# A seven-product block scheme for a quarter-size piece of the main product, with W0 read from DRAM again in every batch

## The chip, the cores and the metric

One core of one Trainium2 chip runs the kernel as a single program. The metric is the device time of one execution in microseconds (us). Five engines matter: PE (matmuls), DVE and ACT (elementwise work, both can read PSUM), POOL (elementwise work in SBUF, and DMAs of its own) and SP (issues most of the DMAs). They run their instruction lists in order and meet at semaphores.

## The reference

Four layers, each added to its input. `x` is 8 batches x 256 tokens x 1024.

```python
# layer 0: a plain weight, and a sign matrix of its own for every batch
x = x + (einsum('bsi,oi->bso', x, W0) + b0 + einsum('bsi,bio->bso', x, 2*mask - 1) * coeff[:, None, None])
# layer 1: a weight that is quantized to a codebook, with a LoRA part
x = x + x @ w_eff.T
# layer 2: a shared weight, bias, and an adapter per batch, chosen by token
x = x + (einsum('bti,oi->bto', x, W2) + b2 + lora(x, A2[tok2[b]], B2[tok2[b]]) * 2.0)
# layer 3: a rank-16 adapter per batch
x = x + einsum('bnr,bor->bno', einsum('bni,bri->bnr', x, B3[tok3[b]]), A3[tok3[b]])
```

## The kernel before

The first 175 us or so build what all batches share. Layers 1 and 2 with their residuals are one 1024x1024 matrix P = (I + W1eff)^T (I + W2)^T, kept as a high part `P_hi` and a low part `P_lo`, both float32r; a product of two such pairs is three matmuls (high-high, high-low, low-high). W0^T plus the identity is written to `w0t_dram` in DRAM and read into SBUF once, as `w0_t` (32 KB of each partition).

Then come eight batches. A batch has two halves on PE.

*Layer 0* (lines 1432 and 1439). The mask arrives as eight row tiles k = 0 to 7, each 128 partitions x 1024 (two k-tiles of 512 output columns), in a ring of four slots. For each row tile ACT turns the mask into signs (`signs`, L730, 1024 wide), DVE adds the tile of W0 (`merged`, L1078, 1024 wide), ACT rounds each half to float32r (`m_hi`, L740, 512 wide, twice) and DVE takes the rest (`m_lo`, L1084, 512 wide, twice). `Mh` and `Ml` are rings of four halves, so a half n waits until PE is through with half n-4. PE works on pairs of halves: eight matmuls of 512 columns with `m_hi` (both halves), then eight of 256 columns with `m_lo`. Halves n = 2k and 2k+1 are row tile k. The output of layer 0 goes through `x1_part` (ACT, L777), `x1_sum` (DVE, L1131), `x1_hi` (ACT, L781) and `x1_lo` (POOL for four tiles, DVE for four).

*Main* (lines 1468 to 1470). Four outputs (2 token halves x 2 column halves of 512) are each the sum over eight k-tiles of three matmuls, 96 matmuls in all. Between them stand eight `rank` matmuls (L1478) and, at the end of each output, one `close` matmul with the adapters (L1485). `out_add` on DVE (L1127) adds the bias to the bank and writes `out_staged` (two slots), and SP stores it.

The order on every engine is written out by hand. ACT stands in `signs(4)`, `signs(5)`, `m_hi(2)`, `m_hi(3)`, `m_hi(4)`, `signs(6)`, `m_hi(5)`, four `x1_part`, `m_hi(6)`, `signs(7)`, `m_hi(7)`. SP issues masks, tables, `x` and stores from one in-order queue, each behind its own wait: mask tile k+4 goes out when `m_lo(k)` has freed the slot, and the next batch's `x` when layer 0 has been read.

Of the kernel before, what the change touches and what calls it, by code (L numbers as in the profile page):

```python
# [30 lines left out]
def cond_resid_chain(nc, x, coeff, codebook, tok2, tok3, mask, w0, b0, w1, scale_log, lora_a, lora_b,  # L31
# [161 lines left out]
    with ExitStack() as ctx:  # L193
        def sem(name):
# [27 lines left out]
        MAIN_BANK = [3, 6, 7, 4]  # L222
        RANK_BANK = 5
# [36 lines left out]
        def _(sp):  # L260
# [1266 lines left out]
```

## Time and profile before

| | |
|---|---|
| median of 3 runs | 557.57 us (557.49 to 558.6) |
| the profiled execution's own time | 557.65 us |
| its span (first to last instruction) | 555.6 us |
| PE busy | 541.3 us, 97% of the span |
| DVE, ACT, POOL busy | 398.2, 328.9 and 157.8 us (72%, 59%, 28%) |
| moved by DMA | 80.07 MB, 144 GB/s over the span |

The profiled execution's time is its span and 2.05 us around it, and it is 0.08 us above the median of the runs. A PE matmul is shown longer than its turn takes, since matmuls overlap: the turn is read from the starts of two that follow each other. A busy share is an average over stages; what an edit in one stage can bring is read from the waits of that stage.

### The profile page before, as it was taken

What the parts mean: (1) busy time and instruction counts of PE and PEld (TensorE: products, weight loads), DVE (VectorE), ACT (ScalarE), POOL (GpSimd) and SP (SyncE); (2) the same over time, 40 slices, a digit from 0 to 9 for tenths busy, and PEclk for the clock granted to TensorE, in tenths of its full rate; (3) what the DMA queues carried; (4) which work ended last, traced back from release to release, by engine and by line L of the source; (5) the groups of instructions that cost most, each with busy time, mean ns of one, the idle gap of its engine ahead of it and who ended that gap; (6) DMA issues with size and microseconds to landing.
All of it is one profiled execution on the core that took longest, in us unless ns stands there. A gap on an engine that the chain in (4) does not pass through costs nothing.

```text
span 555.6 us, 8876 instructions
## 1 busy us (share of the span) xinstructions
PE 541.3 (97%) x2892; PEld 464.6 (84%) x2892; DVE 398.2 (72%) x622; ACT 328.9 (59%) x622; POOL 157.8 (28%) x170
## 2 busy tenths in 40 slices
PE   5999999999999999999999999999999999999997
PEld 4988888888888788888888888888888888888886
DVE  5998898988956859666765875866687487586631
ACT  3877766776655846564564664656557466564620
POOL 2769778987714040021012002102100300210200
PEclk9999999999999999999999999999999999999999
DMA  8766042733577982574475366256447635634202
GB/s 230 246 88 143 21 145 62 248 97 113 120 192 231 314 204 97 170 186 69 149 221 113 132 187 156 63 170 197 76 151 226 114 119 163 174 73 151 76 0 76
DMA packets 138120, 80.07 MB, mean 144 GB/s; under 512 B 95664, under 2 KB 111024, under 8 KB 138096
## 3 DMA queue, kind: packets, MB, share of 16 engines
q1 hardware_dynamic: 137520, 78.71, 51.8%
q0 software_dynamic: 288, 1.05, 0.5%
q8 instruction: 13, 0.21, 0.2%
q14 instruction: 11, 0.09, 0.0%
q10 hardware_dynamic: 288, 0.01, 0.0%
HBM read 65.59 MB, written 14.16 MB: 144 GB/s over the span
## 4 chain that ended last, share of the span: by engine, by line
PE 84%; DVE 8%; ACT 4%; DMA 3%; issue 1%; POOL 0%; DVEq 0%; ACTq 0%; SPq 0%; POOLq 0%
PE bank L1432 19%; PE bank L1468 10%; PE bank L1469 10%; PE bank L1470 10%; PE bank L1439 10%; PE bank L1306 5%; PE bank L1308 5%; PE bank L1307 5%; PE bank L1478 3%; PE bank L1216 2%; PE bank L1485 1%; DVE merged_ring L1078 1%; DVE w_lo L984 1%; DMA mask_ring<-in_mask_Bx4096x_ik 1%; ACT bank L574 1%; PE bank L1230 1%
## 5 line engine op out<-in xcount | busy, mean ns | idle before, releaser
L1432 PE MATMUL bank<-x_t_pair,m_hi 128*128 128x512 f32 x512 | 128.4, 393 | 1.8 <-ACT m_hi L740 1.6
L740 ACT CAST m_hi<-merged_ring 128x512 fp32r<-128x512 f32 x128 | 73.0, 618 | 66.1 <-PE bank L1439 34.1
L1432 PEld LDWEIGHTS bank<-x_t_pair,m_hi 128*128 128x128 f32 x512 | 92.5, 189 | 19.5 <-ACT m_hi L740 2.6
L1084 DVE TENSOR_TENSOR m_lo<-merged_ring,m_hi 128x512 fp32r<-128x512 f32 x128 | 82.4, 689 | 30.7 <-ACT m_hi L740 30.6
L1468 PE MATMUL bank<-P_hi,x_t_pair 128*128 128x512 f32 x256 | 99.7, 389 | 0.0
L1469 PE MATMUL bank<-P_lo,x_t_pair 128*128 128x512 f32 x256 | 99.7, 389 | 0.0
L1470 PE MATMUL bank<-P_hi,x_t_pair 128*128 128x512 f32 x256 | 99.6, 389 | 0.0
L530 POOL TENSOR_TENSOR x_t_pair<-x_sum,x_t_pair 128x256 fp32r<-128x256 f32 x32 | 24.8, 801 | 260.5 <-ACT x_t_pair L781 260.5
L1078 DVE TENSOR_TENSOR merged_ring<-merged_ring,w_t 128x1024 f32<-128x1024 f32 x64 | 78.3, 1234 | 21.6 <-ACT merged_ring L730 20.6
L730 ACT ACTIVATE merged_ring<-mask_ring,batch_now 128x1024 f32<-128x1024 int32 x64 | 77.9, 1241 | 23.1 <-DMA mask_ring<-in_mask_Bx4096x_ik 22.3
L1439 PEld LDWEIGHTS bank<-x_t_pair,m_lo 128*128 128x128 f32 x512 | 69.9, 190 | 5.0
L1439 PE MATMUL bank<-x_t_pair,m_lo 128*128 128x256 f32 x512 | 71.4, 282 | 0.0
L1470 PEld LDWEIGHTS bank<-P_hi,x_t_pair 128*128 128x128 f32 x256 | 48.1, 188 | 10.0
L1468 PEld LDWEIGHTS bank<-P_hi,x_t_pair 128*128 128x128 f32 x256 | 48.1, 188 | 9.8
L1469 PEld LDWEIGHTS bank<-P_lo,x_t_pair 128*128 128x128 f32 x256 | 48.1, 188 | 9.7
L1131 DVE TENSOR_TENSOR x_sum<-x_sum,bank 128x256 f32<-128x256 f32 x64 | 24.2, 417 | 25.8 <-ACT x_sum L777 25.8
L777 ACT ACTIVATE x_sum<-bank,b_cols 128x256 f32<-128x256 f32 x64 | 26.7, 471 | 18.4 <-PE bank L1439 18.4
L1306 PE MATMUL bank<-w_hi 128*128 128x512 f32 (+1 forms) x96 | 35.2, 367 | 0.4 <-DVE P_lo L973 0.4
L1308 PE MATMUL bank<-w_hi,w_lo 128*128 128x512 f32 (+1 forms) x96 | 34.1, 355 | 0.0
L1307 PE MATMUL bank<-w_lo,w_hi 128*128 128x512 f32 (+1 forms) x96 | 34.1, 355 | 0.0
L1127 DVE TENSOR_TENSOR out_staged<-bank,b_rows 128x512 f32<-128x512 f32 x32 | 21.2, 683 | 13.4 <-PE bank L1485 13.4
L574 ACT ACTIVATE bank<-w_raw,scale_recip 128x128 f32<-128x128 f32 x64 | 19.9, 359 | 16.0 <-DVE acc L940 11.6
(152 smaller groups left out, 869.6 us busy)
## 6 DMA issues: line engine op xcount, KB each, us to landing
mask_ring<-in_mask_Bx4096x_ik SPq DMA_DIRECT2D x64, 512.0 KB, 4.5
out<-out_staged SPq DMA_DIRECT2D x32, 256.0 KB, 2.1
w_nat<-in_L_cond_W SPq DMA_DIRECT2D x14, 512.0 KB, 5.1
x_t_squares<-in_x SPq DMA_DIRECT2D x56, 128.0 KB, 2.7
w_raw<-in_L_cond_weight SPq DMA_DIRECT2D x16, 256.0 KB, 4.5
g_batch<-g_dram SPq DMA_DIRECT2D x32, 128.0 KB, 4.5
w0t_dram<-w_out SPq DMA_DIRECT2D x14, 256.0 KB, 2.7
w_t<-w0t_dram SPq DMA_DIRECT2D x6, 512.0 KB, 5.2
```

What stands on the lines that cost most here:

```text
L730: nc.scalar.activation(ring_f[:, k % MR], ring_i[:, k % MR], ACT.Identity, bias=now[:, 1:2], scale=now[:, 0:1]).then_inc(s["s_set"], 1)
L740: nc.scalar.copy(Mh[:, n % MR], ring_f[:, k % MR, h * HALF:(h + 1) * HALF]).then_inc(s["h_set"], 1)
L1078: nc.vector.tensor_tensor(part, part, w0t[:, part_rows(j), part_cols(j)], ALU.add).then_inc(s["v_set"], 1)
L1084: nc.vector.tensor_tensor(Ml[:, n % MR], ring_f[:, k % MR, h * HALF:(h + 1) * HALF], Mh[:, n % MR].bitcast(F32), ALU.subtract).then_inc(s[ ...
L1306: mm(o, hi[:, t], Wh[:, t, c0:c1], start=(t == 0), stop=False)
L1307: mm(o, hi[:, t], Wl[:, t, c0:c1], start=False, stop=False)
L1308: ins = mm(o, lo_[:, t], Wh[:, t, c0:c1], start=False, stop=(t == KT - 1))
L1432: mm(bank[L0_BANK[HT * h + j]][:, :], Mh[:, n % MR, j * P:(j + 1) * P], xThl[:, :, :, k + i, :], start=(k + i == 0), stop=False, skip_grou ...
L1439: ins = mm(bank[L0_BANK[HT * h + j]][:, 0:T], Ml[:, n % MR, j * P:(j + 1) * P], xTh[:, :, k + i, :], start=False, stop=(k + i == KT - 1), ...
L1468: mm(o, x1h[:, k, toks], Ph[:, k, cols], start=(k == 0), stop=False)
L1469: mm(o, x1h[:, k, toks], Pl[:, k, cols], start=False, stop=False)
L1470: mm(o, x1l[:, k, toks], Ph[:, k, cols], start=False, stop=False)
```

## The change

**Main.** In batches 2 to 7, the first four of main's eight k-tiles form a 2 x 2 block product: tokens (two halves of 128) by k (tiles 0 and 1 as X, 2 and 3 as Y), times k by columns (two halves of 512). Done directly it is eight block products; the new `batch` on PE does it with seven. Four sums of rows of P (`t_sum`, made once in batch 1, nine DVE steps of 1024 wide and their high and low parts `t_hi`, `t_lo`) and four sums of the layer-0 output (`s_sum`, four DVE steps of 256 wide per batch, with high parts by `a_hi` on ACT and low parts by `a_lo` on DVE; they lie in the columns 512 to 1023 of P's k-tiles 0 and 1, which the scheme no longer reads) are the new operands. A block product is two k-tiles times three matmuls. Four outputs need partial sums of banks, done by DVE: `c11_seen` and `c22_sums`, two steps of 512 wide each; POOL adds biases to them (`v_bias`, `p_bias`). Batches 0 and 1 keep the plain 96 matmuls. The outputs are now numbered by `OUT = [(0,0), (1,0), (0,1), (1,1)]`, and each of the four is closed in turn, output 3 with 12 matmuls alone.

**W0.** The space of `w0_t` is needed for the T tiles. After batch 0, W0 is not resident: SP reads it again from `w0t_dram` in each of batches 1 to 7, eight loads of 512 KB a batch, into `w0_landing` with two slots. The load of tile j waits until `merged(j-2)` has read the slot.

**Order.** `signs` and `merged` of the next batch's first two row tiles now stand at the end of a batch, ahead of the `u` steps. The stores of the outputs move from SP's queue to POOL's (the last two of batch 7 stay on SP).

```diff
+            def load_w0(b, j):
+                sp.wait_ge(s["v_set"], KT * b + j - 1)
+                sp.dma_start(land[:, j % 2].rearrange("p (i n) -> p i n", i=2),
+                             w0t_dram[part_rows(j), :, part_cols(j)].rearrange("k p n -> p k n")).then_inc(w0_land[j % 2], 16)
+            def load_next(b, last):
                 if not last:
-                    for k in range(MR):
-                        sp.wait_ge(s["m_ready"], 2 * KT * b + 2 * (k + MR) + 2)
-                        load_mask(b + 1, k)
+                    for k in range(MR, KT):
+                        next_mask(b, k)
+                        if k < MR + 2:
+                            load_w0(b + 1, k - MR)
...
+            def batch(b, last=False):
+                load_w0(b, 2)
+                load_w0(b, 3)
+                next_mask(b, 0)
+                next_mask(b, 1)
+                load_w0(b, 4)
+                load_w0(b, 5)
+                load_w0(b, 6)
+                load_w0(b, 7)
+                next_mask(b, 2)
+                next_mask(b, 3)
+                sp.wait_ge(s["out_done"], 4 * b)
+                load_tables(b)
+                load_next(b, last)
...
+            with pool.Fori(3, NB) as b:
+                pool.wait_ge(s["u_done"], b)
+                c_copies(b)
+                v_bias(b - 1)
+                store(b - 1, 0)
+                p_bias(b - 1)
+                for i in range(1, 4):
+                    store(b - 1, i)
+                x1_lo(b)
...
-                nc.vector.tensor_tensor(part, part, w0t[:, part_rows(j), part_cols(j)], ALU.add).then_inc(s["v_set"], 1)
+                if first:
+                    row = w0t[:, part_rows(j), part_cols(j)]
+                else:
+                    dve.wait_ge(w0_land[j % 2], 64 * (b - 1) + 16 * (j // 2 + 1))
+                    row = land[:, j % 2].rearrange("p (i n) -> p i n", i=2)
+                nc.vector.tensor_tensor(part, part, row, ALU.add).then_inc(s["v_set"], 1)
...
+            def batch(b):
+                layer0(b)
+                for kk in range(2):
+                    pe.wait_ge(s["x1_ready0"], HT * b + kk + 1)
+                    ins = product(bank[MAIN_BANK[0]][:, :], x1_of(kk, 0), p_of(kk, 0), start=(kk == 0), stop=(kk == 1))
+                ins.then_inc(s["prod_done"], 1)
+                pe.wait_ge(s["t_ready"], 4)
+                for o, i, j in ((P6_BANK, S2, T2), (MAIN_BANK[2], S1, T1), (MAIN_BANK[1], S3, T3)):
+                    pe.wait_ge(s["a_ready"], 4 * (b - 1) - 3 + i)
+                    for kk in range(2):
+                        ins = product(bank[o][:, :], sum_of(i, kk), t_of(j, kk), start=(kk == 0), stop=(kk == 1))
+                    ins.then_inc(s["prod_done"], 1)
+                rank(b)
+                pe.wait_ge(s["c_sums"], 4 * (b - 1) - 3)
+                for kk in range(2):
+                    product(bank[MAIN_BANK[0]][:, :], x1_of(2 + kk, 0), p_of(2 + kk, 0))
+                main(b, 0, range(HT, KT))
+                close(b, 0)
...
+                main(b, 3, range(HT, KT), True)
+                close(b, 3)
```

Three places of the order. On DVE, the start of a batch up to the middle of layer 0; `merged_ring` with 1024 columns is `merged`, `m_lo` comes in halves, `out_staged` is an `out_add` of the batch before, and `x_t_pair` of 512 is the low part of the transposed `x`. Before (batch 7, its first rows):

```order
L1078 TENSOR_TENSOR merged_ring<-merged_ring,w_t 128x1024
L1097 TENSOR_TENSOR x_t_pair<-x_t_squares,x_t_pair 128x512 x4
L1127 TENSOR_TENSOR out_staged<-bank,b_rows 128x512 x2
L1078 TENSOR_TENSOR merged_ring<-merged_ring,w_t 128x1024
L1084 TENSOR_TENSOR m_lo<-merged_ring,m_hi 128x512 x4
L1078 TENSOR_TENSOR merged_ring<-merged_ring,w_t 128x1024 x2
L1127 TENSOR_TENSOR out_staged<-bank,b_rows 128x512
L1078 TENSOR_TENSOR merged_ring<-merged_ring,w_t 128x1024
L1127 TENSOR_TENSOR out_staged<-bank,b_rows 128x512
L1078 TENSOR_TENSOR merged_ring<-merged_ring,w_t 128x1024
L1084 TENSOR_TENSOR m_lo<-merged_ring,m_hi 128x512 x6
L1078 TENSOR_TENSOR merged_ring<-merged_ring,w_t 128x1024
```

And now, after the loop's branch:

```order
L1200 TENSOR_TENSOR m_lo<-merged_ring,m_hi 128x512 x4
L1251 TENSOR_TENSOR out_staged<-bank,b_rows 128x512
L1251 TENSOR_TENSOR out_staged<-bank,c_sum 128x512
L1213 TENSOR_TENSOR x_t_pair<-x_t_squares,x_t_pair 128x512 x4
L1251 TENSOR_TENSOR out_staged<-bank,c_sum 128x512
L1194 TENSOR_TENSOR merged_ring<-merged_ring,w_landing 128x1024 x2
L1251 TENSOR_TENSOR out_staged<-bank,v_sum 128x512
L1194 TENSOR_TENSOR merged_ring<-merged_ring,w_landing 128x1024 x2
L1200 TENSOR_TENSOR m_lo<-merged_ring,m_hi 128x512 x6
L1194 TENSOR_TENSOR merged_ring<-merged_ring,w_landing 128x1024
```

Moved: the first two `merged` have gone to the end of the batch before; `m_lo(0)` and `m_lo(1)` lead; the third `out_add` stands ahead of `merged(2)`, and the fourth ahead of `merged(4)`.

On SP, the issues of the last batch. Before, in the order of masks 4 and 5, two stores, masks 6 and 7, the tables, then stores:

```order
L336 DMA mask_ring<-in_mask_Bx4096x_ik 128x2x512 x2
L398 DMA out<-out_staged 128x512 x2
L336 DMA mask_ring<-in_mask_Bx4096x_ik 128x2x512 x2
L415 DMA g_batch<-g_dram 32x1024 x4
L398 DMA out<-out_staged 128x512 x4
```

And now, where `w_landing` is W0 (tiles 2 and 3, then 4 to 7):

```order
L422 DMA w_landing<-w0t_dram 128x2x512 x2
L355 DMA mask_ring<-in_mask_Bx4096x_ik 128x2x512 x2
L422 DMA w_landing<-w0t_dram 128x2x512 x4
L355 DMA mask_ring<-in_mask_Bx4096x_ik 128x2x512 x2
L437 DMA g_batch<-g_dram 32x1024 x4
```

Moved: masks 6 and 7 stand behind the W0 loads of tiles 6 and 7, which wait for `merged(4)` and `merged(5)`.

On POOL, one turn of the loop now, where before it held only the four copies and the four `x1_lo`:

```order
L607 ISA
L608 TENSOR_TENSOR v_sum<-v_sum,b_rows 128x512
L602 ISA
L604 ISA
L604 DMA out<-out_staged 128x512
L611 REGISTER_ALU
L612 TENSOR_TENSOR c_sum<-c_sum,b_rows 128x512
L604 ISA
L604 DMA out<-out_staged 128x512
L602 REGISTER_ALU
L604 ISA
```

Added: two adds of 512 wide and the four stores, each behind its own wait.

## Rows read from the trace of the kernel before

**Rows 1.** Page, parts 1 and 2: busy time by engine, granted clock in 40 slices
```profile
PE 541.3 (97%) x2892; PEld 464.6 (84%) x2892; DVE 398.2 (72%) x622; ACT 328.9 (59%) x622; POOL 157.8 (28%) x170
...
PEclk9999999999999999999999999999999999999999
```

**Rows 2.** Waits of PE from 150 us on: total, times, longest
```profile
PE bank L1432 <- ACT m_hi L740: 1.6, 2, 1.2
```

**Rows 3.** Timeline of PE, one whole batch: start us, us, line, tiles, count
```profile
318.07 1.98 PE L1432 MATMUL bank<-x_t_pair,m_hi 128*128 128x512 f32 x8
...
337.60 2.00 PE L1432 MATMUL bank<-x_t_pair,m_hi 128*128 128x512 f32 x8
...
347.67 0.39 PE L1468 MATMUL bank<-P_hi,x_t_pair 128*128 128x512 f32 x1
...
364.67 0.39 PE L1485 MATMUL bank<-g_batch,u_batch 128*128 128x512 f32 x1
...
364.90 0.62 PE L1432 MATMUL bank<-x_t_pair,m_hi 128*128 128x512 f32 x2
```

**Rows 4.** Page, part 5: two groups of the second half, busy and mean | idle
```profile
L1131 DVE TENSOR_TENSOR x_sum<-x_sum,bank 128x256 f32<-128x256 f32 x64 | 24.2, 417 | 25.8 <-ACT x_sum L777 25.8
...
L777 ACT ACTIVATE x_sum<-bank,b_cols 128x256 f32<-128x256 f32 x64 | 26.7, 471 | 18.4 <-PE bank L1439 18.4
```

**Rows 5.** Timeline at the end: last closing matmul and the sum behind it
```profile
551.98 0.39 PE L1485 MATMUL bank<-g_batch,u_batch 128*128 128x512 f32 x1
...
552.40 0.69 DVE L1127 TENSOR_TENSOR out_staged<-bank,b_rows 128x512 f32<-128x512 f32 x1 [4.97 <-PE bank L1485]
```

**Rows 6.** Timeline of DVE and SP around the start of that batch
```profile
308.67 1.28 DVE L1127 TENSOR_TENSOR out_staged<-bank,b_rows 128x512 f32<-128x512 f32 x2
...
313.51 2.36 DVE L1078 TENSOR_TENSOR merged_ring<-merged_ring,w_t 128x1024 f32<-128x1024 f32 x2
...
321.21 1.30 DVE L1084 TENSOR_TENSOR m_lo<-merged_ring,m_hi 128x512 fp32r<-128x512 f32 x2 [0.51 <-ACT m_hi L740]
...
322.68 0.41 SPq L336 DMA_DIRECT2D mask_ring<-in_mask_Bx4096x_ik  x1
...
349.27 0.43 DVE L1180 TENSOR_TENSOR u_batch<-u_sum,u_batch 32x256 fp32r<-32x256 f32 x1 [0.47 <-ACT u_batch L819]
```

**Rows 7.** Landings, by tile: masks issued at 312.5, 313.6, 220.0 and 337.5
```profile
DMA to landing us min/median/max: 3.9/3.9/3.9
...
DMA to landing us min/median/max: 4.5/4.5/4.5
...
DMA to landing us min/median/max: 5.5/5.5/5.5
...
DMA to landing us min/median/max: 3.6/3.6/3.6
```

**Rows 8.** Landings, by tile: three W0 loads at 174.5 to 175.5, under load
```profile
DMA to landing us min/median/max: 4.3/4.5/6.0
```

**Rows 9.** Landings, by tile: output stores from SP, then the POOL gathers
```profile
DMA to landing us min/median/max: 2.0/2.1/2.8
...
L499 POOL DMA_INDIRECT b_nat<-in_L_cond_lora_Bs,table_rows x1: 958/958/958, 25.4 to 25.4; - x1
...
DMA to landing us min/median/max: 4.4/5.8/7.1
```

**Rows 10.** Timeline of ACT and PE in batch 0, where PE waited
```profile
188.87 1.25 ACT L730 ACTIVATE merged_ring<-mask_ring,batch_now 128x1024 f32<-128x1024 int32 x1 [0.42 <-DMA mask_ring<-in_mask_Bx4096x_ik]
...
196.34 1.14 ACT L740 CAST m_hi<-merged_ring 128x512 fp32r<-128x512 f32 x2 [1.57 <-DVE merged_ring L1078]
...
197.02 2.11 PE L1432 MATMUL bank<-x_t_pair,m_hi 128*128 128x512 f32 x8 [0.38 <-ACT m_hi L740]
```

**Rows 11.** Timeline of ACT in the steady batch of rows 3
```profile
332.78 1.24 ACT L730 ACTIVATE merged_ring<-mask_ring,batch_now 128x1024 f32<-128x1024 int32 x1
...
335.39 1.14 ACT L740 CAST m_hi<-merged_ring 128x512 fp32r<-128x512 f32 x2 [1.36 <-DVE merged_ring L1078]
```

More of the change, by code:

```diff
@@ L808, in batch @@
                     x1_hi(b, o)
+                if not first and not second:
+                    a_hi(b)
                 x1_part(b, HT)
@@ L814, in batch @@
                     x1_hi(b, o)
+                if not last:
+                    coef_now(b + 1)
+                    for k in range(2):
+                        signs(b + 1, k)
                 act.wait_ge(s["u_done"], b + 1)
@@ L819, in batch @@
                 nc.scalar.copy(Us[:, :], usum[:, :]).then_inc(s["u_hi"], 1)
+                if not last:
+                    y_now(b + 1)
             act.wait_ge(s["late_in"], 32)
             batch(0, first=True)
-            with act.Fori(1, NB - 1) as b:
+            batch(1, second=True)
+            batch(2, third=True)
+            with act.Fori(3, NB - 1) as b:
                 batch(b)
@@ L1168, in batch @@
                         merged(b, KT - 1, first)
+                        if second:
+                            t3_part()
+                        if not plain:
+                            a_sums(b)
+                if second:
+                    t3_sum()
+                if not plain:
+                    a_lo(b)
                 x1_sum(b, HT)
@@ L1173, in batch @@
                     x1_lo(b, o)
+                if not plain:
+                    c11_seen(b)
                 if not last:
-                    x_turn(b + 1, range(1))
+                    for k in range(2):
+                        merged(b + 1, k, False)
                 dve.wait_ge(s["u_part"], b + 1)
@@ L1180, in batch @@
                 nc.vector.tensor_tensor(Us[rows, :], usum[rows, :], Us[rows, :].bitcast(F32), ALU.subtract).then_inc(s["u_ready"], 1)
+                if not plain:
+                    dve.wait_ge(s["u_ready"], b + 1)
+                    c22_sums(b)
                 if not last:
-                    x_turn(b + 1, range(1, 2))
+                    x_turn(b + 1)
+                if second:
+                    for i in (T1, T2):
+                        t_lo(i)
             batch(0, first=True)
             batch(1, second=True)
-            with dve.Fori(2, NB - 1) as b:
+            batch(2, third=True)
+            with dve.Fori(3, NB - 1) as b:
                 batch(b)
             batch(NB - 1, last=True)
-            for t in range(2):
-                for h in range(2):
-                    out_add(NB - 1, t, h)
+            for i in range(4):
+                out_add(NB - 1, i)
         @block.tensor
@@ L1500, in _, with plain_batch @@
-            batch(0, first=True)
-            with pe.Fori(1, NB - 1) as b:
+                mm(bank[MAIN_BANK[i]][:, :], Us[:, t * P:(t + 1) * P], Gs[:, h * HALF:(h + 1) * HALF], start=False, stop=True, skip_group_check=True).then_inc(s["out_done"], 1)
+            def plain_batch(b):
+                layer0(b, b == 0)
+                for i in range(2):
+                    main(b, i, range(HT), True)
+                rank(b)
+                for i in range(2):
+                    main(b, i, range(HT, KT))
+                for i in range(2):
+                    close(b, i)
+                for i in range(2, 4):
+                    main(b, i, range(KT), True)
+                    close(b, i)
```

299 lines of the change are left out of this document (227 added, 72 removed).

## Prediction

> **What bounds the kernel now.** I read the page first: PE is busy 97% of the span at full granted clock [rows 1]. Then PE's waits after 150 us: 1.6 us in two waits, the later of them at 197 in batch 0 [rows 2, 10]. In the batches PE is a wall, and nothing but its own matmuls is on the path. Then PE's timeline of one batch [rows 3]: layer 0 starts at 318.07 and the next at 364.90, so a batch is 46.83 us. From 347.67 to 364.67 stand 75 matmuls of 512 columns, 0.2267 us each, and the eight pairs of layer 0 come every (337.60-318.07)/7 = 2.79 us. DVE and ACT have slack that the change spends: 25.8 and 18.4 us in eight batches, 3.2 and 2.3 us each, right ahead of the second half of `x1` [rows 4]. A second slack matters more. `m_hi(7)` starts at 335.39, its first half (0.6 us) is done at 336.0, and PE wants it at 337.60: 1.6 us to spare in a batch [rows 3, 11]. The reader is to see that this is the thinnest cover in layer 0.
>
> **What PE gains.** Before: 96 main matmuls. Now 6 + 18 ahead of `rank`, then three times 6 + 12, then 12: 90. Six fewer in each of six batches: 36 x 0.2267 = 8.16 us, 1.36 a batch.
>
> **What hides at no cost.** The four `s_sum` steps and four `a_lo` on DVE (256 wide, 0.35 each, 2.8 in all) and four `a_hi` on ACT (1.3) go into the gaps of 3.2 and 2.3 us of rows 4. If all that cover were gone, `rank` would wait up to 2.8 us a batch; today PE has 24 matmuls (5.4 us) between layer 0 and `rank`, and still has. `c11_seen` and `c22_sums`, four steps of 0.6, follow `x1_lo`, where PE asks for the first one only at the end of `rank`. `signs` and `merged` for two tiles move forward, into idle time of both engines.
>
> **The new chain through layer 0.** This is the price. Take S as the start of layer 0 of batch b, 3 to 7; PE wants half n = 14 (row tile 7) at S + 19.53 [rows 3]. W0 has two slots and masks four, so the stream of tiles is now a ring of loads, and its clock starts late. Step by step:
> - `close` of output 2 stands 14 matmuls ahead of S: -3.17. The sum behind a close starts 0.42 later [rows 5]: the third `out_add` at -2.75. The next step follows 0.6 later [rows 6]: `merged(2)` at -2.15. Two `merged` take 2.36 [rows 6]: `merged(2)` ends near -0.95, `merged(3)` at +0.2.
> - SP issues 0.17 after its release (322.51 to 322.68 [rows 6]). W0 for tile 4 goes out at -0.8, for tile 5 at +0.4.
> - No row shows a W0 load in a steady batch. Masks of the same 512 KB do: 3.9 for one with nothing near it, 3.6 at best, 4.5 for one issued 1.2 us behind another, 5.5 in batch 1 [rows 7]; W0 itself 4.3 to 6.0 in a busy stretch [rows 8]. Tile 5 is a load 1.2 us behind another: 4.5, and 0.3 more (my estimate, between nothing and the 1.0 that separates 4.5 from 5.5) for a store of POOL at its side. It lands at 5.2.
> - `merged(5)` ends at 6.4. Only then comes `m_lo(2)`, a pair of 1.3 [rows 6]: 7.6. Its first half is wanted at S + 5.58 + 1.81 = 7.4, so PE may already lose 0.1 to 0.4.
> - The mask of tile 6 goes out at 7.8, 1.2 behind W0 of tile 7. I take 4.8 (4.5, and 5.5 in the early batch): 12.6. Before, it was issued at S + 4.6 [rows 6].
> - From the start of `signs(6)` to that of `m_hi(7)`, with ACT and DVE running through and nothing else late, batch 0 took 196.34-188.87 = 7.47, and PE started 0.68 later [rows 10]. In this stretch stand `m_hi(5)`, four `x1_part`, `m_hi(6)`, `signs(7)` and `merged(7)`, as they do now. Half 14 is worked on at 12.6 + 8.15 = 20.75, which is 1.2 late. A restart costs 0.13 more (2.11 for eight matmuls, not 1.98 [rows 3, 10]), and there are two: **1.5 us a batch**.
>
> 1.5 against 1.36: batches 3 to 7 come out +0.14 each, +0.7 in all.
>
> At this place the Trainium skill speaks against me. Its page "DMA: Bandwidth & Descriptors", section "Anatomy of one DMA — SWDGE (gpsimd) path", gives a DMA as about 2.0 us and bytes over 436 GB/s, 3.2 us for 512 KB. The rows never show less than 3.6. By the page both landings would be over 1.3 us shorter, the ring would be hidden, and the sum would be the second rival's below.
>
> **Batch 2** follows a plain batch, whose third close stands 26 matmuls ahead of S, at -5.9, so the chain has 2.7 us more: no stall, -1.36.
>
> **Batch 1** saves no matmul. It starts 2.7 us earlier too, but DVE does the nine steps for T, 1.15 each. Three lie ahead of `m_lo(2)` beyond what the landing hides: from `merged(3)` at -2.55, two T steps to -0.3, `out_add` to 0.9 (released by the close at S), `merged(4)`, one, `merged(5)`, one, `m_lo(2)`: 6.8, so mask 6 goes out at 7.0. With 5.2 (nearer the 5.5 of the early batch) it lands at 12.2; one T step stands between `merged(6)` and `m_lo(5)`: 12.2 + 8.15 + 1.15 = 21.5, 2.0 late and 0.1 for the restart. **+2.1.** Bounds: 0.8 with 3.9, and 3.0 with 6.0.
>
> **Sum.** 557.65 of the profiled execution - 1.36 + 0.7 + 2.1 = **559.1 us**; the median is 0.08 lower, which changes nothing. Bounds of the likeliest case: the two landings from 4.3 and 4.3 to 5.5 and 5.5 give a stall of 0.7 to 2.9, so five times -0.7 to +1.5; with batch 1's 0.8 to 3.0 and batch 2 between -1.36 and nothing: 553.8 to 568.
>
> **The rivals.**
> - *The loads land as they do alone* (3.9 and 3.9, or less). Mask 6 lands at 10.8, half 14 at 19.0: no stall in batches 2 to 7. 557.65 - 8.16 + 0.8 = 550.3; with one of the two short, 552 to 555. It decides below a sum of both landings of 8.2 us, where 1.5 sinks under 0.3. For it: 3.6 and 3.9 are what lone masks show. Against: both loads are second in a pair. This ends on the other side, at 551. The page's rule above gives this case too.
> - *POOL's stores come late.* The third `out_add` needs slot 0 back from the first store. u ends 2.0 after `rank` [rows 3, 6], then DVE has 1.3 for `c22_sums`, 2.3 for two transposes, 2.4 for four `m_lo` and 0.7 for the `out_add`, 8.7 in all; `rank` ends 70 matmuls ahead of S, at -15.87, so the store goes out at -7.1 and has 4.3 us. SP's stores took 2.1; POOL's gathers of twice the size held POOL 0.96 and landed in 4.4 and 7.1 [rows 9]. At 4.3 or less it costs nothing; at 6 it moves the ring by 1.7 in five batches: 559.1 + 8.5 = 568, at 7.1 it is 573.
> - *DMA saturates.* W0 adds eight loads of 512 KB, 4 MB, to the same 4 MB of masks. If steady landings were the 6.0 of rows 8, both 1.3 longer: 559.1 + 6 x 2.5 = 574 and more.
> - *Exactly even*: not a mechanism but the crossing of the first two, 556.5 to 558.7.
>
> **How the numbers follow.** The main case 0.47, loads that land early 0.37, POOL's stores 0.12, saturation 0.04. A measurement of this kernel can tell about 0.2%, 1.1 us. Of the main case 0.12 falls within that, 0.01 below; of the second 0.02 within. Faster 0.36, same 0.14, slower 0.50. The time is that of the main case, 559.1; the range, 550.5 to 568, leaves out the best tenth and the late stores and saturation.
>
> **What the profile after would show.** PE's waits name `m_hi` (the first of eight at half 14, 0.8 to 1.5 us a batch) and `m_lo` at halves 4 and 5. ACT idles before `signs(6)` for its mask, near S + 12.6. DVE idles before `merged(5)` for W0, landing near S + 5.2. Batch 2 takes 45.5, batches 3 to 7 about 47.0, batch 1 about 48.9. Main has 90 matmuls at the same 0.2267 each. I am wrong if the wait is somewhere else: `a_ready`, `c_sums` or `rank`'s `x1` would mean that the cover of rows 4 was misjudged; `out_add` waiting for a store is the third case; no waits at all, the second.

## The result and the profile after

The changed kernel takes 592.37 us (median of 4, 587.88 to 595.03) and the kernel before 557.53 (557.3 to 558.6): ratio 1.061, 95% interval 1.055 to 1.068. The forecast was 559.1, range 550.5 to 568. It missed the time by 33 us. The profiled run took 592.46, span 590.7.

Page of the changed kernel, parts 1, 2 and 5, to set beside [rows 1, 4]:

```profile
PE 545.0 (92%) x2856; PEld 461.5 (78%) x2856; DVE 460.2 (78%) x707; ACT 340.7 (58%) x658; POOL 203.6 (34%) x213
...
PEclk9999999999999999899999989999998999999999
...
L1659 PE MATMUL bank<-x_t_pair,m_hi 128*128 128x512 f32 x512 | 133.4, 403 | 13.0 <-ACT m_hi L827 12.8
...
L1666 PE MATMUL bank<-x_t_pair,m_lo 128*128 128x256 f32 x512 | 75.2, 289 | 18.5 <-DVE m_lo L1200 18.5
```

The 36 matmuls are gone (2892 to 2856), but PE is no wall any more: it waits in layer 0, at `m_lo` and at `m_hi`, and three slices of its granted clock fall under nine tenths. Its waits from 150 us on, beside [rows 2] (total, times, longest):

```profile
PE bank L1666 <- DVE m_lo L1200: 18.5, 7, 4.2
PE bank L1659 <- ACT m_hi L827: 12.8, 14, 2.0
...
PE bank L1697 <- POOL x_t_pair L584: 0.4, 1, 0.4
```

Seven waits for `m_lo`: one in each of batches 1 to 7. None for `a_ready`, `c_sums` or `rank`. So all but 0.4 us of the waiting is in layer 0, where the forecast looked, and its size was wrong. From the start of one layer 0 to the next, read off the timelines:

| us in batch | 1 | 2 | 3 | 4 | 5 | 6 | 7 |
|---|---|---|---|---|---|---|---|
| before | 46.83 | 46.82 | 46.83 | 46.83 | 46.83 | 46.83 | 46.83 |
| changed | 54.87 | 49.81 | 51.88 | 51.36 | 52.51 | 49.98 | 51.57 |
| forecast | 48.9 | 45.5 | 47.0 | 47.0 | 47.0 | 47.0 | 47.0 |

Timeline of the changed kernel around layer 0 of batch 5, which starts at S = 433.24:

```profile
427.93 3.79 DVE L1213 TENSOR_TENSOR x_t_pair<-x_t_squares,x_t_pair 128x512 fp32r<-128x512 f32 x4
428.07 0.56 POOL L604 DMA_DIRECT2D out<-out_staged  x1 [4.54 <-DVE out_staged L1251]
428.66 1.30 POOL L612 TENSOR_TENSOR c_sum<-c_sum,b_rows 128x512 f32<-128x512 f32 x1
...
432.54 0.69 DVE L1251 TENSOR_TENSOR out_staged<-bank,c_sum 128x512 f32<-128x512 f32 x1 [0.81 <-DMA out<-out_staged]
...
434.39 9.01 SPq L422 DMA_DIRECT2D w_landing<-w0t_dram  x4
...
440.44 2.57 DVE L1194 TENSOR_TENSOR merged_ring<-merged_ring,w_landing 128x1024 f32<-128x1024 f32 x2 [4.34 <-DMA w_landing<-w0t_dram]
...
442.93 3.69 DVE L1200 TENSOR_TENSOR m_lo<-merged_ring,m_hi 128x512 fp32r<-128x512 f32 x6
...
443.67 1.34 PE L1666 MATMUL bank<-x_t_pair,m_lo 128*128 128x256 f32 x8 [2.86 <-DVE m_lo L1200]
...
444.37 1.59 SPq L355 DMA_DIRECT2D mask_ring<-in_mask_Bx4096x_ik  x2
...
450.76 1.24 ACT L817 ACTIVATE merged_ring<-mask_ring,batch_now 128x1024 f32<-128x1024 int32 x1 [5.10 <-DMA mask_ring<-in_mask_Bx4096x_ik]
451.91 1.12 ACT L827 CAST m_hi<-merged_ring 128x512 fp32r<-128x512 f32 x2
...
452.56 3.49 PE L1659 MATMUL bank<-x_t_pair,m_hi 128*128 128x512 f32 x8 [1.97 <-ACT m_hi L827]
```

Read it downward: it is the chain of the forecast, link for link, and each link is late. The third `out_add` starts at S - 0.7; W0 of tile 4 goes out at S + 1.1; `merged(4)` starts at S + 7.2 and idled 4.3 for it; `m_lo(2)` only follows `merged(5)`, and PE waits for it at half 4 (443.67); mask 6 goes out at S + 11.1; ACT idles 5.1 for it; PE gets half 10 at 452.56, where 13.95 from S would be 447.2. The start is late on two counts. DVE ends the low part of `x` (`x_t_pair`, four steps) at 431.72, S - 1.5, and so could not have begun the third `out_add` at the forecast's S - 2.75. Then it idles 0.81 for the slot that store 0 gives back. The landings, by tile (W0 of tiles 4 and 5, mask 6, store 0), beside [rows 7, 8, 9]:

```profile
DMA to landing us min/median/max: 6.0/6.1/6.2
...
DMA to landing us min/median/max: 6.4/6.4/6.4
...
DMA to landing us min/median/max: 4.3/4.3/4.3
```

And the windows of the stretch up to the end of PE's second wait, of the eight matmuls behind it, and of the rest of the batch (columns: us, busy of PE, PEld, DVE, ACT, POOL, granted clock, DMA's share, GB/s):

```profile
443.60:452.50 8.90, 6.92 (x40) 5.98 (x40) 3.40 (x7) 2.96 (x5) 0.00 (x0) 1.00 0.91 273
452.50:455.80 3.30, 3.24 (x8) 2.57 (x9) 3.30 (x8) 3.30 (x9) 0.00 (x0) 0.56 1.01 208
455.80:485.70 29.90, 29.90 (x143) 25.22 (x142) 27.08 (x43) 19.82 (x37) 10.06 (x12) 0.99 0.74 207
```

Behind the second stall PE ran eight matmuls in 3.49 us and not 1.98, at a granted clock of 0.56, near the lower of its two levels (1.2 of 2.4 GHz). The lower level was granted once in each of batches 1, 3 and 5. In batches 2, 4, 6 and 7 PE waited up to 2.80 us and ran on at full clock. Two windows, behind a wait of 2.86 in batch 3 and behind one of 2.80 in batch 7:

```profile
340.30:343.60 3.30, 3.18 (x12) 2.89 (x13) 2.98 (x6) 1.24 (x2) 0.00 (x0) 0.50 0.84 260
546.20:549.50 3.30, 3.30 (x20) 2.91 (x21) 2.85 (x5) 1.17 (x2) 0.00 (x0) 1.00 0.91 287
```

### The profile page after: what moved, and what is told of

It is laid out like the page before. It is cut to its first block, busy times and chain, and to the rows that moved or that the text cites. A ratio compares the mean times of both kernels' runs of the same rounds, so it can differ in the third digit from the quotient of the medians.

```text
span 590.7 us, 9024 instructions
## 1 busy us (share of the span) xinstructions
PE 545.0 (92%) x2856; PEld 461.5 (78%) x2856; DVE 460.2 (78%) x707; ACT 340.7 (58%) x658; POOL 203.6 (34%) x213
## 4 chain that ended last, share of the span: by engine, by line
DVE 29%; PE 25%; DMA 23%; ACT 9%; issue 8%; SPq 2%; POOL 1%; DVEq 1%; ACTq 0%; POOLq 0%
DMA mask_ring<-in_mask_Bx4096x_ik 10%; DVE merged_ring L1194 8%; DVE m_lo L1200 8%; DMA w_landing<-w0t_dram 7%; PE bank L1533 5%; PE bank L1535 5%; PE bank L1534 5%; DMA out<-out_staged 4%; ACT merged_ring L817 3%; DVE P_lo L1306 3%; DVE x_sum L1327 2%; SPq L350 2%; DMA b_nat<-in_L_cond_B,table_rows 1%; PE bank L1443 1%; ACT x_t_pair L882 1%
## 5 line engine op out<-in xcount | busy, mean ns | idle before, releaser
L1659 PE MATMUL bank<-x_t_pair,m_hi 128*128 128x512 f32 x512 | 133.4, 403 | 13.0 <-ACT m_hi L827 12.8
L1194 DVE TENSOR_TENSOR merged_ring<-merged_ring,w_landing 128x1024 f32<-128x1024 f32 x56 | 68.0, 1234 | 56.2 <-ACT merged_ring L817 31.0
L1666 PE MATMUL bank<-x_t_pair,m_lo 128*128 128x256 f32 x512 | 75.2, 289 | 18.5 <-DVE m_lo L1200 18.5
L584 POOL TENSOR_TENSOR x_t_pair<-x_sum,x_t_pair 128x256 fp32r<-128x256 f32 x32 | 31.1, 1002 | 170.9 <-ACT x_t_pair L882 170.9
L1697 PE MATMUL bank<-P_hi,x_t_pair 128*128 128x512 f32 x160 | 62.5, 391 | 0.4 <-POOL x_t_pair L584 0.4
L1698 PE MATMUL bank<-P_lo,x_t_pair 128*128 128x512 f32 x160 | 62.3, 389 | 0.0
L1699 PE MATMUL bank<-P_hi,x_t_pair 128*128 128x512 f32 x160 | 62.3, 389 | 0.0
L604 POOL DMA_DIRECT2D out<-out_staged x30 | 16.5, 551 | 89.8 <-DVE out_staged L1251 89.8
L1697 PEld LDWEIGHTS bank<-P_hi,x_t_pair 128*128 128x128 f32 x160 | 30.0, 188 | 7.3 <-POOL x_t_pair L584 1.2
L1699 PEld LDWEIGHTS bank<-P_hi,x_t_pair 128*128 128x128 f32 x160 | 30.0, 188 | 6.3
L1698 PEld LDWEIGHTS bank<-P_lo,x_t_pair 128*128 128x128 f32 x160 | 30.0, 188 | 6.1
L882 ACT CAST x_t_pair<-x_sum 128x256 fp32r<-128x256 f32 x64 | 23.5, 402 | 14.1 <-DVE x_sum L1327 13.8
L661 ACT ACTIVATE bank<-w_raw,scale_recip 128x128 f32<-128x128 f32 x64 | 19.9, 359 | 15.8 <-DVE acc L1051 11.1
L576 POOL CAST c_batch<-C_hi 128x256 fp32r (+1 forms) x24 | 14.9, 656 | 40.3 <-PE bank L1711 40.3
```

Of the source, the lines that this page charges most:

```text
L1194: nc.vector.tensor_tensor(part, part, row, ALU.add).then_inc(s["v_set"], 1)
L1659: mm(bank[L0_BANK[HT * h + j]][:, :], Mh[:, n % MR, j * P:(j + 1) * P], xThl[:, :, :, k + i, :], start=(k + i == 0), stop=False, skip_grou ...
L1666: ins = mm(bank[L0_BANK[HT * h + j]][:, 0:T], Ml[:, n % MR, j * P:(j + 1) * P], xTh[:, :, k + i, :], start=False, stop=(k + i == KT - 1), ...
L1697: mm(o, x1h[:, k, toks], Ph[:, k, cols], start=(start and k == ks[0]), stop=False, skip_group_check=True)
L1698: mm(o, x1h[:, k, toks], Pl[:, k, cols], start=False, stop=False, skip_group_check=True)
L1699: mm(o, x1l[:, k, toks], Ph[:, k, cols], start=False, stop=False, skip_group_check=True)
```

## The experiments

Beside the changed kernel, twelve more ran, each against the kernel before (its medians were 557.95, 557.83 and 557.31 in the three groups). The letters in the expectations: theory A is that the written order makes a chain of loads whose links add up.

| kernel | us | ratio, 95% interval |
|---|---|---|
| changed | 592.4 | 1.061, 1.055 to 1.068 |
| m_lo first and masks early | 559.35 | 1.002, 1.000 to 1.004 |
| stores on SP | 589.6 | 1.055, 1.052 to 1.059 |
| both of these | 559.5 | 1.002, 0.999 to 1.005 |
| W0 loaded once | 554.2 | 0.993, 0.991 to 0.995 |
| DVE's order alone | 587.2 | 1.052, 1.051 to 1.054 |
| SP's order alone | 582.0 | 1.044, 1.041 to 1.048 |
| no products, ring kept | 571.0 | 1.025, 1.021 to 1.028 |
| before, stores on POOL | 559.2 | 1.003, 1.002 to 1.004 |
| signs(6) behind m_hi(5) | 582.6 | 1.045, 1.043 to 1.048 |
| merged(2), (3) before out_add | 574.3 | 1.031, 1.029 to 1.034 |
| first, and T spread | 555.85 | 0.997, 0.994 to 0.999 |
| first, T spread, merged early | 552.9 | 0.991, 0.989 to 0.993 |

### The order on DVE and SP, both halves

```diff
+                    m_lo(b, 2)
                     merged(b, MR, first)
...
+                    m_lo(b, 3)
                     merged(b, MR + 1, first)
...
-                load_w0(b, 6)
-                load_w0(b, 7)
                 next_mask(b, 2)
+                load_w0(b, 6)
                 next_mask(b, 3)
+                load_w0(b, 7)
```

> The changed kernel with DVE's m_lo(2) ahead of merged(4) and m_lo(3) ahead of merged(5), and SP's loads in the order mask 6, W0 of tile 6, mask 7, W0 of tile 7. Nothing is added or left out. Theory A (order): the loss is the written order, in which mask 6 waits for m_lo(2), and m_lo(2) waits on DVE behind merged(5) and its W0 landing. Here mask 6 goes out at about S + 4.5 and no longer at S + 11, lands before S + 11, and both the wait of PE for m_lo at halves 4 and 5 (18.5 us in all) and that for m_hi at half 10 (12.8 us) go; the stretches at 0.43 us per matmul behind them go too. 592.4 - 18.5 - 12.8 - about 8 = 553 us, range 551 to 560. Theory B (stores): the third out_add, late behind POOL's store, sets the chain whatever the order; then m_lo(2) is still late by up to 1 us and W0 of tile 5 sets halves 10 and 11: 565 to 580. Theory C (bandwidth): landings grow to more than 6 us as loads lie closer together: over 580.

559.35 us: inside theory A's range, outside the others'. 33 of the 35 us come back by moving two steps of DVE and two loads of SP past others. Its waits of PE from 276 us on (batches 2 to 7), then the windows of batches 1 and 4:

```profile
PE bank L1662 <- ACT m_hi L827: 0.6, 1, 0.6
```

```profile
226.08:277.88 51.80, 48.56 (x238) 39.83 (x237) 43.66 (x59) 31.09 (x52) 8.32 (x12) 1.00 0.79 209
...
369.69:415.16 45.47, 45.47 (x232) 38.82 (x231) 41.12 (x62) 28.85 (x52) 10.99 (x15) 1.00 0.82 242
```

Batch 4 takes 45.47, which is 46.83 - 1.36: the whole gain of six matmuls, with all sums, `a_lo`, `c11` and `c22` hidden. DMA moves 242 GB/s there and PE waits for nothing. So neither the products nor the DMA's rate is the bound. What is left is mostly batch 1, 51.8; batches 2, 3, 5 and 7 took 0.4 to 1.0 more than 45.47.

### One half at a time

DVE's half alone, the first two of the + lines above:

> The changed kernel with DVE's half of the reordering alone: m_lo(2) ahead of merged(4), m_lo(3) ahead of merged(5). SP still issues W0 of tiles 6 and 7 ahead of masks 6 and 7. Theory A has two links: m_lo late behind merged(5), and mask 6 late. This mends the first alone: the waits for m_lo at halves 4 and 5 (18.5 us) go, but mask 6 now waits on SP behind W0 of tile 7, whose slot comes free with merged(5) near S + 9, so it goes out at about S + 9.3 and lands at S + 15: half 14 is some 2 to 3 us late, 1 us of it in a slow stretch. 557.9 - 8.2 + 6 x 2.8 + 5 for batch 1 = 571 us, range 565 to 580. Rival: SP's order is nothing, DVE's is all: 559 as with both; or DVE's is nothing: over 585.

SP's half alone, the rest:

> The changed kernel with SP's half of the reordering alone: mask 6, W0 of tile 6, mask 7, W0 of tile 7; DVE's order stays, with m_lo(2) behind merged(5). DVE's half alone gave 587.2 and both halves 559.4. If the two are links of one chain (theory A), SP's half alone gives as little: mask 6 is still held until m_lo(2) is done near S + 10, and W0 of tile 6 now waits behind it: 585 to 600 us, 590 the likeliest. Rival (SP's order was the fault, DVE's no part of it): 560 to 570.

587.2, outside my range, and 582.0, 3 us below the range. Neither does it alone. PE's waits with DVE's half, then with SP's half:

```profile
PE bank L1662 <- ACT m_hi L827: 25.4, 12, 4.7
PE bank L1669 <- DVE m_lo L1200: 1.8, 1, 1.8
```

```profile
PE bank L1666 <- DVE m_lo L1200: 17.9, 7, 3.5
PE bank L1659 <- ACT m_hi L827: 3.0, 4, 1.1
```

With DVE's half the wait for `m_lo` is down to 1.8 and the one for `m_hi` has doubled: mask 6 stands on SP behind W0 of tile 7, whose slot comes free with `merged(5)`. I had put that at S + 9.3; in batches 3, 5 and 7 it was 11.2 to 11.5, as late as in the changed kernel. With SP's half the wait for `m_lo` stays, but mask 6, no longer in the company of W0 of tiles 6 and 7, lands in 4.1 to 4.5 us where it took 5.3 to 6.4 in batches 2 to 7, and the wait for `m_hi` falls to 3.0. That is what I missed: the order also decides what shares the DMA with a load.

### The output stores

POOL's stores are taken out, and stores 0, 1 and 2 of SP stand behind masks 4 and 5, store 3 behind W0 of tile 5:

```diff
                 next_mask(b, 1)
+                for i in range(3):
+                    store(b - 1, i)
                 load_w0(b, 4)
                 load_w0(b, 5)
+                store(b - 1, 3)
```

> The changed kernel with all output stores back on SP's queue, each placed by its time (stores 0, 1, 2 behind masks 4 and 5, store 3 behind W0 of tile 5); POOL keeps its two bias adds. Theory A: the store is the first link of the chain and the order the rest. A store of SP lands in about 2.1 to 2.8 us and not 4.35, so the third out_add goes from S - 0.7 to about S - 2.5; the chain behind it is 1.8 earlier in batches 3 to 7, so 592.4 - 5 x 1.8 - some 3 us of slow matmuls = 580 us, range 575 to 585. Theory B (the stores are the whole of it: slot, POOL's port and queue): 553 to 565. Rival C (SP's queue gets longer and W0 of tile 5 waits behind a store's release): no gain, 590 or more.

> The two edits of the runs beside it together: stores on SP, m_lo(2) and m_lo(3) ahead of merged(4) and merged(5), mask 6 ahead of W0 of tile 6. Theory A: with mask 6 out early there is no wait of PE in batches 2 to 7; it comes near the before's time less six batches x 1.36 us, plus some for batch 1: 557.5 - 8.2 + 1 = 550.5 us, range 549 to 555. Theory B: the same to within 1 us as the kernel with the stores alone. Rival (DVE is the bound: 2.8 us of sums and a_lo and the stretched two-operand steps): 556 or more.

589.6 and 559.5: almost nothing, and nothing on top of the order. Both lie outside theory A's ranges (575 to 585 and 549 to 555). The second fell where the rival "DVE is the bound" had put it, at 556 or more; but of its excess 7.4 us stand in batch 1 (54.2), and batches 2 to 7 took 45.9 to 46.5. The landing of store 0 in batch 5 shows why my 2.1 to 2.8 was wrong:

```profile
DMA to landing us min/median/max: 5.8/5.8/5.8
```

It was issued 0.7 us behind mask 5, 1.9 behind mask 4, and landed in 5.8. In batches 3 to 7 store 0 took 5.6 to 6.2 from SP here and 4.3 to 5.4 from POOL in the changed kernel; in the kernel before SP's stores had no load of 512 KB just ahead of them (2.1 [rows 9]). The late slot is real, but the queue it is issued from is not what makes it late. The two masks at its side are: with no load of W0 at all (the kernel of "The loads of W0") store 0 still took 4.3 to 6.3. The page "Trainium Kernel Development and Optimization" of the Trainium skill, section "Key Constraints", says that DMAs of SP, ACT and POOL run on the same 16 engines and interleave. These runs agree in that a store behind the masks was late from either queue, 5.6 to 6.2 us by SP and 4.3 to 5.4 by POOL. The kernel before with its stores moved to POOL was the control:

> The kernel before, with its output stores issued by POOL and no longer by SP; nothing else is changed. Theory A: POOL's stores cost nothing in themselves, each slot is wanted again 12 us or more after its store: 557.9 us, within 0.3%. Rival B (POOL's stores disturb DVE or land late): 560 or more, and DVE's out_add waits for them.

It took 1.3 us more, 0.25%, so my 0.3% held. Its batches still take 46.83 and `out_add` never waits. The difference lies behind the last matmul: 5.2 us to the end of the span and not 3.4. The changed kernel issues its last two stores from SP and has 3.4.

### The loads of W0

```diff
-                        if k < MR + 2:
+                        if k < MR + 2 and isinstance(b, int) and b == 0:
                             load_w0(b + 1, k - MR)
...
-                load_w0(b, 2)
                 ... (3 to 7 likewise)
```

> The changed kernel with the two landing slots of W0 filled once and not again (the 48 further loads of 512 KB are left out, so merged adds the wrong tile and the output is not the reference's). All else stays: products, sums, T, POOL's stores, order. Theory A: merged waits for no load, so the chain through layer 0 loses its two W0 landings; mask 6 goes out near S + 4.5, and PE waits for nothing in batches 3 to 7: 550 to 553 us. Rival D (the sums on DVE and ACT, the late store or POOL's port cost PE its time): what stays above 551 is theirs; 560 or more if they are the main part.

The kernel leaves out 54 of the 56 loads of W0, so `merged` adds the wrong tile. 554.2, 1 us above the range. Window of batch 5, then the landing of mask 6 in it:

```profile
412.16:457.62 45.46, 45.46 (x231) 38.81 (x230) 40.35 (x61) 28.86 (x52) 10.16 (x15) 1.00 0.55 150
```

```profile
DMA to landing us min/median/max: 3.8/3.8/3.8
```

In batches 2 to 7 PE waits for nothing (45.47 to 45.51), and mask 6 lands in 3.8, not 6.4. Batch 1 still takes 51.4, without a load of W0 in it: something other than the ring costs that batch 4.6 by itself.

### The ring without the products

DVE, ACT, PE and POOL on the plain path in every batch, the order and W0's loads as they are:

```diff
-            for b in range(2):
+            plain_batch(0)
+            with pe.Fori(1, NB - 1) as b:
                 plain_batch(b)
```

> The changed kernel with all batches on the plain 96 products: no seven products, no T, no s_sum, a_lo, a_hi, c11 and c22 sums and no bias adds on POOL. W0 still comes from DRAM in every batch, in the changed kernel's order on DVE and SP, and POOL still stores the outputs. The result is the reference's by the old formula. Theory A (the ring in its written order is the loss, the products are free): batches 1 to 7 take what batch 2 took in the changed kernel, which also follows a plain batch, plus the six matmuls: 49.8 + 1.36 = 51.2, less some for DVE's lighter load; 557.9 + 7 x 4 = 586 us, range 575 to 590. Rival D (the sums, the products' waits and T are a large part): under 570.

571.0, a miss: batches 2 to 7 took 48.3 in the mean, 1.45 over 46.83, where I had expected 4.4 over, from batch 2 of the changed kernel and six matmuls. The third `out_add` starts at S - 3.5 to - 4.6 here and at S - 0.1 to - 0.7 in batches 3 to 7 of the changed kernel. So the ring alone costs 1.45 a batch in that order, and 5.7 in the changed kernel (34.3 us over six times 45.47). The seven products are not free after all in this order: the chain starts about 3 us later with them. It isn't the third close that does it, which stands 14 matmuls ahead of S and not 26: no third `out_add` waits for its close in either kernel. DVE is what differs. Here are its low part of `x` and the third `out_add` in batch 5, whose S is 420.69:

```profile
411.39 2.49 DVE L1193 TENSOR_TENSOR x_t_pair<-x_t_squares,x_t_pair 128x512 fp32r<-128x512 f32 x4
417.05 0.69 DVE L1231 TENSOR_TENSOR out_staged<-bank,b_rows 128x512 f32<-128x512 f32 x1 [3.17 <-DMA out<-out_staged]
```

DVE is done with `x` at S - 6.8, and at S - 1.5 to - 2.3 in the changed kernel. Store 0 goes out at S - 9.1 and not at S - 5.2 to - 5.9. This run takes away the sums on DVE and the adds on POOL together, so it doesn't say what each of them costs. And batch 1 took 52.3 here, 5.4 over, without one step for T: the ring in its written order is enough for most of the 8.0 that the batch lost.

### Two links, one at a time

```diff
-                    if k == MR:
+                    if k == (MR if first else MR + 1):
                         signs(b, MR + 2)
...
-                    if not first and k == MR:
+                    if not first and k == MR + 1:
                         merged(b, MR + 2, first)
```

> The changed kernel with signs(6) behind m_hi(5) on ACT and merged(6) behind m_lo(5) on DVE, in batches 1 to 7. In the changed kernel PE waits at half 10, though tile 5 had been merged long before: m_hi(5) stands behind signs(6), which waits for mask 6. Theory A': that queue place costs the part of the wait that lies between halves 10 and 12. Here halves 10 and 11 are on time, the wait comes at half 12, 2.8 us of matmuls later, for the same mask: 1.0 to 1.5 us less a batch, seven batches, 592.4 - 9 = 583 us, range 578 to 588. Rival (the wait is for mask 6 wherever it stands, the later ones grow by what the first loses): 590 to 594.

```diff
-                    out_add(b - 1, 2, old)
                     merged(b, 2, first)
                     merged(b, 3, first)
+                    out_add(b - 1, 2, old)
```

> The changed kernel with one move: DVE does merged(2) and merged(3) ahead of the third out_add and not behind it, in the 2 to 3 us in which it idles there for the slot that store 0 gives back. W0 of tiles 4 and 5 go out about 2.3 us earlier. Theory A (a chain whose start sets it): m_lo(2) and mask 6 are about 2 us earlier, less what landings lose by lying closer to masks 4 and 5 and stores 0 and 1: 6 batches x 1.8 + some slow matmuls = 592.4 - 12 = 580 us, range 574 to 586. Rival (DMA's rate is the limit, starting earlier only lengthens the landings): 588 or more.

582.6 (583 expected) and 574.3 (580, at the low end of 574 to 586). PE's waits in the first, then in the second:

```profile
PE bank L1666 <- DVE m_lo L1200: 17.8, 7, 3.1
PE bank L1659 <- ACT m_hi L827: 2.7, 5, 1.0
```

```profile
PE bank L1659 <- ACT m_hi L827: 12.4, 14, 2.7
PE bank L1659 <- DVE out_staged L1251: 2.5, 4, 0.8
...
PE bank L1666 <- DVE m_lo L1200: 0.2, 1, 0.2
```

In the first, half 10 no longer waits behind a load that its tile doesn't need: 10 us of 35. In the second, W0 of tiles 4 and 5 go out earlier, by 6.0 in batch 1, 3.6 in batch 2 and 1.5 to 2.6 in the others (19.6 in all), and the wait for `m_lo`, 18.5 us, is gone: 18 of 35, about the sum of the shifts. What starts the chain earlier comes back nearly in full, in the sum; by batch it does not (batch 3 gained 2.8 for a shift of 1.6, batch 4 0.4 for 2.2).

### A version that beats both

On top of the first experiment, T's steps leave layer 0 of batch 1. Two stand ahead of the second half of x1, two behind `x1_lo`, two at the batch's end, the rest likewise in batch 2, which stays plain:

```diff
+                if second:
+                    t1_parts()
+                if third:
+                    t4_sum()
+                    t3_part()
...
+                if second:
+                    t1_sum()
+                    t2_part()
+                if third:
+                    t3_sum()
...
-            for b in range(2):
+            for b in range(3):
                 plain_batch(b)
```

> The kernel with m_lo(2) and m_lo(3) first and masks 6 and 7 early (its batches 2 to 7 took 45.5 to 46.5, its batch 1 51.8), and on top of it the nine steps for T taken out of layer 0 of batch 1: DVE does two of them ahead of the second half of x1, two behind x1_lo and two at the end of batch 1, three in the same places of batch 2, ACT's four t_hi likewise, and batch 2 stays on the plain 96 products, so only batches 3 to 7 save six matmuls. Theory A (the rest of the loss is the place of T's steps in batch 1, on DVE and in front of m_hi on ACT): batch 1 takes 47 to 47.5, batch 2 46.8, batches 3 to 7 45.5 to 46: 557.9 - 5 x 1.36 + about 1.5 = 552.5 us, range 551 to 555. Rival (batch 1 is slow since its W0 loads and masks share DMA with batch 1's stores and tables, or since DVE has no room for T anywhere): 555 to 559, with waits in batches 1 and 2.

And this with `merged(2)` and `merged(3)` ahead of the third `out_add`:

> The kernel with T's steps spread and masks 6 and 7 early (555.85 median, 552.5 to 560.6), with the same move on top: merged(2) and merged(3) ahead of the third out_add. What was left in it: the wait at half 14 for W0 of tile 7, 0.3 to 1.0 us in batches 1, 3 and 7, and 0.5 in one batch for the third out_add. Theory A: tiles 4 to 7 of W0 come 1 to 2.3 us earlier, these waits go, and the spread with them: 557.8 - 6.8 + 1.3 for the stores on POOL + 0.5 = 553 us, range 551.5 to 554.5. Rival (the DMA rate): 555.5 as without it.

555.85 (12 runs, 552.5 to 560.6): 0.85 above the range; batch 1 fell from 51.8 to 48.8. Then 552.9 (6 runs, 551.7 to 554.3), 0.9% faster than the kernel before, interval 0.7 to 1.1%, and 6.7% faster than the changed kernel. Windows of its batches 4 and 5, then two of its waits:

```profile
366.04:411.83 45.79, 45.76 (x232) 38.74 (x231) 40.38 (x61) 28.80 (x52) 10.81 (x14) 1.00 0.83 241
411.83:457.29 45.46, 45.46 (x231) 38.81 (x230) 40.45 (x61) 28.75 (x52) 10.24 (x14) 1.00 0.84 243
```

```profile
PE bank L1665 <- ACT m_hi L827: 2.5, 2, 2.1
...
DVE out_staged L1256 <- DMA out<-out_staged: 2.0, 3, 1.0
```

Both waits of PE for `m_hi` lie in batch 0, as in [rows 2]: in batches 1 to 7 PE waits for it nowhere. DVE's three waits for a store stand in batches 1 to 3.

## Why the prediction was wrong

**The mechanism was right, its price was not.** The forecast had a stall of 1.5 us in each of batches 3 to 7; it was 4.5 to 7.0. Batch 5 against the steps, in us from S:

| step | forecast | measured |
|---|---|---|
| store 0 goes out, lands | -7.1, 2.1 later | -5.2, 4.3 later |
| third `out_add` | -2.75 | -0.70 |
| W0 of tile 5 out | 0.4 | 2.28 |
| it lands | 5.2 | 8.45 |
| PE goes on at half 4 | 7.4 to 7.8 | 10.4 |
| mask 6 out | 7.8 | 11.13 |
| it lands | 12.6 | 17.50 |
| half 10 | 13.95, no wait | 19.3 |
| half 14 | 20.75 | 26.6 |

26.6 - 19.53 is 7.0, the loss of batch 5 against 45.47. For the first point below, three rows from the end of batch 4, where `merged` of the next batch now stands:

```profile
416.94 2.55 DVE L1194 TENSOR_TENSOR merged_ring<-merged_ring,w_landing 128x1024 f32<-128x1024 f32 x2
417.68 0.45 ACT L924 ACTIVATE u_sum<-bank,batch_now 128x256 f32<-128x256 f32 x1
419.41 0.41 DVE L1398 TENSOR_TENSOR u_sum<-u_sum,bank 128x256 f32<-128x256 f32 x1
```

- **"The third `out_add` at -2.75"** is the first failed step. I set it by the close of output 2 alone. It started at -0.70, 2.05 later: 1.2 of that is DVE itself, and 0.81 the wait for the slot. I had `signs` and `merged` for two tiles move "into idle time of both engines". In the trace DVE has no idle time there: the two `merged` stand ahead of `u_sum`, whose input ACT had ready at 418.13, and `u` comes 1.3 late. The low part of `x` then takes 3.79 and not 2.49, beside POOL's `p_bias`. So DVE is free at -1.5, where the forecast's own steps make it about -4.1. The store was a rival, "POOL's stores come late", at 0.12, with 4.3 us to spare from -7.1. It went out 1.9 later than that: DVE was late, and POOL issued it 0.65 after its release, where SP takes 0.17. It took 4.3, where I priced it by SP's 2.1 [rows 9], a store with no other load beside it. SP's queue in its place is no better. These shares are read from the trace of batch 5; no run took them apart.
- **The landings, 4.8 and 4.8**, were 6.2 and 6.4, together 3.0 more (5.0 to 6.2 and 5.3 to 6.4 over batches 3 to 7). "DMA saturates" had the 6.0 of [rows 8] at 0.04. I took rows of the kernel before, in which a load has at most one other of 512 KB near it; now a batch has 16 loads of 512 KB and not 8, and they go out in pairs (DMA's share is 0.76 over batch 5, 0.52 before). As a bound on the whole the rate was rightly dismissed: at 243 GB/s the last version does not wait. In the order written, though, it lengthens every link. The 3.2 us for 512 KB, an estimate from the fit of the Trainium skill (page "DMA: Bandwidth & Descriptors", section "Anatomy of one DMA — SWDGE (gpsimd) path", made for DMAs that POOL issues), is further off still; SP's loads show 3.6 at best.
- **"Half 14"** was the wrong place to look, the step on [rows 10, 11]. `m_hi(5)` stands behind `signs(6)` on ACT, and `m_lo(5)` behind `merged(6)` on DVE. Mask 6 landing at 12.6, my own number, plus 1.2 and 0.6, already gives half 10 at 14.4, past 13.95. The run with both moved gave 10 us.
- **The stalls add.** I let one wait stand for the ring. PE lost 3.0 at half 4, 2.1 at half 10 and 1.9 in slow matmuls behind them. Over batches 2 to 7 gaps of over 0.3 us make 27.5 and slower matmuls 6.9 of the 34.3, of which 3.1 fall in the two stretches at the lower clock, in batches 3 and 5; the clock was not in the forecast at all.
- **Batch 2, "no stall, -1.36"**: +3.0. Batch 1, its predecessor, is plain, but two steps of `t_lo` (2.3 us) stand on DVE ahead of it. Store 0 went out at S - 7.3 and took 5.55, DVE idled 2.9 for it, and the third `out_add` started at S - 1.6, not - 5.5.
- **Batch 1, +2.1**: +8.0. With the order mended it is still +5.0, and without W0's loads +4.6; 3.0 of that goes when T's steps are spread. In the written order the ring alone costs batch 1 5.4, without T, so the two losses overlap. I charged three of nine steps. ACT's `t_hi`, which stands ahead of `m_hi` and idled 3.1 and 3.3 us for DVE's sums in batch 1 of the mended order, was not charged.
- **What was right**: 36 matmuls at 0.2267, the sums hidden from PE ([rows 4] held; 0.4 us of waiting for x1 in the whole run), though not from DVE's part of the chain, and the place and order of the links.

The sum by measured terms: batches 3 to 7 +23.1, batch 2 +3.0, batch 1 +8.0, together 34.2 of the 34.8 between the two profiled runs. Two small sums of the forecast were off and changed nothing: a landing of 6.0 is 1.2 and not 1.3 over 4.8, and two landings of 4.3 give a stall of 0.5 by its steps, not 0.7.

What stays open is how the length of a landing follows from its neighbours. The runs show 3.8, 4.3, 4.8 and 6.4 for mask 6 of the same size, but no run varied the neighbours one by one. Nor is the company all of it. In batches 3 to 7 of the changed kernel W0 of tile 4 goes out with the same neighbours at the same distances (store 2 goes out 0.5 ahead of it, W0 of tile 5 1.1 and store 3 2.4 behind it). It landed in 5.9 to 6.0 in batches 3, 5 and 7, and in 3.9 in batches 4 and 6. Here are the same 2 us, from S + 3, of batch 5 and of batch 6; the last two columns say that the DMA engines were as busy and moved less than half as much:

```profile
436.24:438.24 2.00, 2.00 (x12) 1.70 (x11) 0.00 (x0) 0.63 (x2) 0.54 (x1) 1.00 0.90 135
488.76:490.76 2.00, 2.00 (x12) 1.69 (x11) 0.12 (x1) 0.64 (x2) 0.54 (x1) 1.00 0.84 295
```

No run says why. Batches 4 and 6 lost 5.9 and 4.5 us, and batches 3, 5 and 7 lost 6.1 to 7.0.

## What to carry to other kernels

A prefetch that becomes a ring through slots is a chain, and its price is not one link's lateness: write down for each load what must retire before its slot is free, what stands ahead of it on every queue, and which loads are in flight with it, and take the landing from a row with the same company. Ask of the chain's first link too what stands ahead of it on its own engine: here DVE, and not the bank it reads, set the start. Where an instruction waits for a load, look at what stands behind it on its engine and doesn't need that load. Moving two such steps on DVE and two on SP was worth 33 of 35 us here, and each half alone 5 and 10.

## What the hardware showed

- A load's landing grows with its company. 512 KB: 3.6 to 3.9 with nothing near it, 4.1 to 4.8 with little beside it, up to 6.4 with two to three others and up to 10.0 in the busiest stretches, but 3.9 at times with the same neighbours. 256 KB: 2.0 from SP and 2.3 from POOL with nothing near it, 5.6 to 6.2 and 4.3 to 5.4 behind two masks.
- DVE's four `x_lo` took 3.79 us in batch 5 beside POOL's sum of 1.30, where four take 2.48 without it: one of them was longer by the whole POOL instruction (1.99 for 0.69). The page "SBUF — State Buffer" of the Trainium skill, section "SBUF: two separate sides", states that a DVE operation with two SBUF inputs and a GpSimd one that reads SBUF exclude each other for the whole instruction; 2.48 + 1.30 = 3.78 agrees.
- A stall of PE can cost more than itself. Behind waits of 4.21, 2.86 and 1.97 us in batches 1, 3 and 5 of the changed kernel the clock was granted at its lower level for a stretch; in batch 5 the next eight matmuls took 3.5 us and not 2.0. Behind waits of up to 2.80 in batches 2, 4, 6 and 7 it stayed at the upper one.
